# A four-layer conditioned residual stack: shifts 2 and 9 as small fp32 tiles, tiles of one width together, full copies ahead of high halves

## The chip, the cores and the metric

One NeuronCore of a Trainium2 chip runs the whole program. The metric is device time in microseconds, as the median of several runs; lower is better. The engines are named as in the profile: PE is TensorE (matmuls), PEld its weight loads, ACT is ScalarE, DVE VectorE, POOL GpSimd, SP SyncE, which issues the DMAs.

## What is computed

The input x is 128 samples of 128 channels by 2048 time steps, in fp32. Four layers follow one another, each added to its own input:

```
x = x + mix(x, cond; L0)     # agg_w[b] @ x + agg_b[b],  agg_w[b] = sum_k att[b,k] * weight[k],
                             # att = softmax(two gelu layers and a linear one on cond)
x = x + conv(x, cond; L1)    # grouped 1-d convolution, 4 groups of 32 channels, 9 taps, pad 4,
                             # plus c_weight @ cond and a bias
x = x + mix(x, cond; L2)
x = x + conv(x, cond; L3)
```

The residual is folded into the weights (an identity is added to each mixing matrix and to the centre tap).

## The kernel before

**Layout.** Layers 0 and 1 work on y1, the output of the first mix, and so on: y1 (after layer 0), y2 (after layer 1), y3 (after layer 2), o (after layer 3). For the convolutions time is split into 4 phases (t = 4m + p), so that a tile is 128 channels by 4 phases by 512 columns, with a halo column at either side. A convolution's output has the partitions (phase, channel of the group), 4 x 32, and one PSUM bank for each of the 4 channel groups. With 9 taps and 4 phases there are 12 shifts s = 0 to 11; shift s feeds output phase p where 0 <= s - p < 9. So shifts 3 to 8 feed all four phases, shifts 2 and 9 three, 1 and 10 two, 0 and 11 one.

**Two kinds of matmul in a convolution.** `dense` (L347 to L363) handles the shifts in `DENSE`, 2 to 9: value and weight are each split in a high and a low part of the type fp32r, and three products are summed (`PASSES`: high x high, high x low, low x high). Each matmul has 32 rows (one channel group) and 128 columns (all phases), and streams 512 columns; the four channel groups lie in the four row groups of the array. That is 8 shifts x 3 passes x 4 groups = 96 matmuls. `sparse` (L332 to L345) handles the shifts in `SPARSE`: plain fp32, 32 rows by 64 columns (two phases), from the unsplit copies `y1_full` and `y3_full`, in two lots: shifts 1 and 10, then shifts 0 and 11 (of whose 64 columns half meet zero weights). Each lot is 4 groups x 2 units = 8 matmuls, which use the whole array, and each fp32 matmul stands in the trace as two instructions. Below, a "pass" is one of these two over all tiles of a lot, so a lot has two passes.

**A step.** Samples are pipelined three deep. `steps`, a hardware loop (`Fori`, i = 3 to 125) and `last_steps` run `step(i)`. On PE it has this order, which nothing but the code's order sets: `first_mix(i)` (fp32, 128x128, 4 matmuls = 8 instructions, L314) into banks 0 to 3; layer 3's convolution of sample i-2, sparse lots first, then dense, into banks 4 to 7; `second_mix(i-1)` (48 fp32r matmuls of 32x128, L329) into banks 0 to 3; layer 1's convolution of sample i, dense first, then the sparse lots, into banks 4 to 7.

**The other engines in a step.** ACT reads banks: `high(1, i-1)` writes the four high parts of y2 (L477), then, for each of four banks of the first mix, a full copy (L476) and a high part (L477) of y1, then `o_ph` (L514, four banks of layer 3), then a full copy and a high part of y3 for each of four banks. DVE subtracts: the low parts of y2 straight from the banks (`low_from_bank`, L609), those of y1 and y3 from the full copies (`low`, L615), and builds the next mixing matrices between (`matrix`, L573 and L578, twice in a step; `halves`, L585 and L587). SP regroups o by 16 DMAs in a step, loads `m_parts`, x, and stores. POOL copies biases and puts o in order of time.

**Semaphores.** `high_set[l]`, `low_set[l]`: counts of high and low parts written of layer l. `mm[l]`: banks finished. Bank 4+t is free for layer 3's convolution when `low_set[1]` has counted t+1 low parts of y2, since DVE reads the bank last (`free3`, L369). A bank of the first mix may be overwritten by the second when `high_set[0]` has counted it, a bank of the second mix by the next first mix when `high_set[2]` has.

At the program's end `last_regroup` (L415) moves the last o by 16 fp32 matmuls of 32x32 tiles, and at its start `keep_busy` (L256) issues filler matmuls.

Of the kernel before, what the change touches and what calls it, by code (L numbers as in the profile page):

```python
# [5 lines left out]
def build_cond_resid(nc, x, small, mix_w, mix_b, conv_w, consts, scratch, out):  # L6
# [7 lines left out]
    PH = 4  # L14
    G = 4
# [8 lines left out]
    DENSE = range(2, SHIFTS - 2)  # L24
    SPARSE = (((1, 0, 2), (10, 2, 2)),
              ((0, 0, 2), (11, 2, 2)))
# [5 lines left out]
    with ctx:  # L32
# [12 lines left out]
        y3_full = sb("y3_full", [128, PH, HALO])  # L45
        o_ph = sb("o_ph", [128, G, N])
# [87 lines left out]
        full_first = sem("full_first")  # L134
# [117 lines left out]
        def _(pe):  # L252
# [26 lines left out]
            keep_busy(3)  # L279
# [12 lines left out]
            def side_bias():  # L292

                pe.wait_ge(ctx_in, 16)
                pe.wait_ge(full_first, 2)
# [7 lines left out]
            def first_mix(i, inner):  # L303
# [7 lines left out]
                for q in range(G):  # L311
                    if inner or i >= 2:
                        pe.wait_ge(high_set[2], nth(i - 2, q))
                    nc.tensor.matmul(ps[:, q, :], m_sum[0][:], x_t[:, q, :], start=True, stop=True).then_inc(mm[0], 1)  # L314

            def second_mix(i, inner):

                pe.wait_ge(m_in, 16 * G * i)
                for g in range(G):
                    pe.wait_ge(low_set[1], nth(i - 1, g))  # L320
                    for n, (m, a) in enumerate(PASSES):
                        first, final = g == 0 and n == 0, g == G - 1 and n == len(PASSES) - 1
                        for p in range(PH):
                            rows = slice(CG * p, CG * (p + 1))
                            if first and has(i, inner, 0):
                                pe.wait_ge(high_set[0], nth(i, p))
                            elif first:
                                pe.wait_ge(high_set[2], nth(i - 2, p))
# [37 lines left out]
            def step(i, inner):  # L366
                now, last, before = has(i, inner, 0), has(i, inner, 1), has(i, inner, 2)

                def free3(t):  # L369
                    if last:  # L370
# [4 lines left out]
                def free1(t):  # L375
                    if before:
                        pe.wait_ge(phases_set, nth(i - 2, t))
                    elif last:
# [19 lines left out]
                if now:  # L398
# [5 lines left out]
                    if not inner and i == 0:  # L404
                        side_bias()
                        pe.wait_ge(full_first, G)
# [18 lines left out]
        def _(act):  # L425
# [43 lines left out]
            def high(layer, j, k, src, dst, full=None):  # L469
# [4 lines left out]
                column = bias[layer][:, k % WIDTH[layer]:k % WIDTH[layer] + 1]  # L474
                if full is not None:
                    nc.scalar.activation(full, src, ACT.Identity, bias=column)  # L476
                nc.scalar.activation(dst, src, ACT.Identity, bias=column).then_inc(high_set[layer], 1)  # L477

            def full_of_first():

                for q in range(G):
                    act.wait_ge(low_set[0], q + 1)
                    nc.scalar.activation(segment(y1_full, q), by_phase(q), ACT.Identity, bias=bias[0][:, 0:1]).then_inc(full_first, 1)

            def step(i, inner):
                now, last, before = has(i, inner, 0), has(i, inner, 1), has(i, inner, 2)
                if last:
                    if inner or i > 1:
                        act.wait_ge(mm[2], 4 * (i - 1))
                    for g in range(G):  # L490
                        high(1, i - 1, g, ps[:, 4 + g, :], y2[:, HIGH, g, :])
                if not inner and i == 0:
                    for q in range(G):
                        high(0, i, q, by_phase(q), segment(y1[:, HIGH], q))
# [301 lines left out]
```

## Time and profile before

| what | value |
|---|---|
| median of 3 runs | 2832.29 us (2830.95 to 2833.19) |
| the profiled execution, time | 2832.44 us |
| the same, span in the trace | 2830.7 us |
| PE busy | 2809.9 us (99%) |
| DVE / ACT / POOL busy | 1961.1 / 1833.8 / 865.7 us |
| dense matmuls (L361) | 24576, 1504.8 us busy |
| sparse matmuls (L343) | 8192 instructions, 509.0 us busy |
| first mix (L314), second mix (L329) | 473.6 us, 384.1 us |
| HBM traffic | 126 GB/s over the span |

Busy shares are averages over the span. "Idle before" is the time an engine stood still ahead of a group, with what ended that. In the timeline, several instructions of one form are merged in one line with their count; its length runs to a modelled end of the last matmul, which laps over the next line's start, so stages are best measured from start to start.

### The profile page before, as it was taken

What the parts mean: (1) busy time and instruction counts of PE and PEld (TensorE: products, weight loads), DVE (VectorE), ACT (ScalarE), POOL (GpSimd) and SP (SyncE); (2) the same over time, 40 slices, a digit from 0 to 9 for tenths busy, and PEclk for the clock granted to TensorE, in tenths of its full rate; (3) what the DMA queues carried; (4) which work ended last, traced back from release to release, by engine and by line L of the source; (5) the groups of instructions that cost most, each with busy time, mean ns of one, the idle gap of its engine ahead of it and who ended that gap; (6) DMA issues with size and microseconds to landing.
All of it is one profiled execution on the core that took longest, in us unless ns stands there. A gap on an engine that the chain in (4) does not pass through costs nothing.

```text
span 2830.7 us, 101562 instructions
## 1 busy us (share of the span) xinstructions
PE 2809.9 (99%) x40052; PEld 1951.1 (69%) x40052; DVE 1961.1 (69%) x2327; ACT 1833.8 (65%) x3101; POOL 865.7 (31%) x1039
## 2 busy tenths in 40 slices
PE   9999999999999999999999999999999999999998
PEld 6667766776677667766776677667766776677665
DVE  6677667766776677667766776677667766776674
ACT  5666666666666666666666666666666666666664
POOL 1233223322332233223322332233223322322332
PEclk9999999999999999999999999999999999999999
DMA  4555555555555555555555555555555555555554
GB/s 138 172 181 179 170 169 181 179 170 169 183 176 170 169 182 177 170 169 182 177 170 170 181 177 170 170 181 178 170 171 180 178 170 171 179 178 170 171 180 139
DMA packets 228036, 489.68 MB, mean 173 GB/s; under 512 B 47016, under 2 KB 129072, under 8 KB 195376
## 3 DMA queue, kind: packets, MB, share of 16 engines
q1 hardware_dynamic: 228016, 489.39, 54.6%
q8 instruction: 15, 0.25, 0.0%
q14 instruction: 5, 0.04, 0.0%
HBM read 205.04 MB, written 150.99 MB: 126 GB/s over the span
## 4 chain that ended last, share of the span: by engine, by line
PE 99%; ACT 1%; DVE 0%; issue 0%; DVEq 0%; ACTq 0%
PE ps L361 52%; PE ps L343 17%; PE ps L314 16%; PE ps L329 13%; ACT y L477 0%; ACT y_full L476 0%; PE ps L256 0%; PE ps L261 0%; PE ps L298 0%; DVE x_t L653 0%; PE ps L415 0%; DVE y L609 0%; ACT L438 0%; DVE conv_parts L548 0%; ACT o_ph L514 0%
## 5 line engine op out<-in xcount | busy, mean ns | idle before, releaser
L361 PE MATMUL ps<-y,conv_parts 32*128 32x512 f32 x24576 | 1504.8, 392 | 1.3 <-DVE y L609 1.0
L361 PEld LDWEIGHTS ps<-y,conv_parts 32*128 32x128 f32 x24576 | 1301.0, 183 | 235.5 <-issue 105.7
L477 ACT ACTIVATE y<-ps,bias 128x512 fp32r<-128x512 f32 x1536 | 1051.4, 712 | 368.8 <-PE ps L343 355.5
L615 DVE TENSOR_TENSOR y<-y_full,y 128x512 fp32r<-128x512 f32 x1020 | 797.5, 810 | 432.4 <-ACT y L477 432.3
L685 POOL COPY bias<-bias_table 128x4 f32 (+3 forms) x512 | 199.6, 404 | 1945.3 <-DMA o_ch<-o_ph 1324.5
L476 ACT ACTIVATE y_full<-ps,bias 128x512 f32<-128x512 f32 x1020 | 733.7, 719 | 26.7 <-PE ps L329 25.0
L691 POOL COPY o_t<-o_ch 128x512 f32<-128x512 f32 x508 | 691.4, 1483 | 10.1 <-DMA o_ch<-o_ph 10.1
L514 ACT ACTIVATE o_ph<-ps,bias 128x512 f32<-128x512 f32 x510 | 309.3, 689 | 581.5 <-PE ps L361 581.5
L609 DVE SCALAR_TENSOR_TENSOR y<-ps,bias,y 128x512 fp32r<-128x512 f32 x516 | 351.8, 744 | 373.8 <-ACT y L477 373.7
L343 PE MATMUL ps<-y_full,conv_raw 32*64 32x512 f32 x8192 | 509.0, 601 | 6.6 <-ACT y L477 4.9
L314 PE MATMUL ps<-x_t,m_sum 128*128 128x512 f32 x1024 | 473.6, 605 | 0.6 <-ACT bias_table L467 0.6
L573 DVE TENSOR_TENSOR prod<-mix_sb,att_table 128x1152 f32<-128x1152 f32 x254 | 416.6, 1640 | 0.0
L329 PE MATMUL ps<-y,m_parts 32*128 32x512 f32 x6144 | 384.1, 392 | 2.3 <-ACT y L477 2.3
L314 PEld LDWEIGHTS ps<-x_t,m_sum 128*128 128x128 f32 x1024 | 184.0, 189 | 287.5 <-issue 287.5
L578 DVE TENSOR_REDUCE m_sum<-prod 128x128 f32<-128x1152 f32 x256 | 346.4, 1353 | 20.2
L343 PEld LDWEIGHTS ps<-y_full,conv_raw 32*64 32x64 f32 x8192 | 151.9, 130 | 279.3 <-issue 179.1
L329 PEld LDWEIGHTS ps<-y,m_parts 32*128 32x128 f32 x6144 | 300.5, 184 | 62.9 <-ACT y L477 2.9
L587 DVE TENSOR_TENSOR m_own<-m_sum,m_own 128x128 fp32r<-128x128 f32 x128 | 37.4, 292 | 4.4
L585 DVE CAST m_own<-m_sum 128x128 fp32r<-128x128 f32 x128 | 29.1, 227 | 15.8
L648 DVE TENSOR_SCALAR o_ph<-ps,bias 128x512 f32<-128x512 f32 x2 | 1.4, 746 | 8.9 <-PE ps L361 8.9
L256 PE MATMUL ps<-y 128*128 128x512 f32 x12 | 5.6, 596 | 1.5 <-DVE y L590 1.5
L457 ACT ACTIVATE bias_table<-ps,room 128x128 f32<-128x128 f32 x8 | 2.3, 491 | 6.2 <-PE ps L298 6.2
(53 smaller groups left out, 59.0 us busy)
## 6 DMA issues: line engine op xcount, KB each, us to landing
x_t<-x SPq DMA_DIRECT2D x128, 1024.0 KB, 5.0
o_ch<-o_ph SPq DMA_DIRECT2D x2032, 64.0 KB, 2.0
out<-o_t SPq DMA_DIRECT2D x127, 1024.0 KB, 3.9
m_parts<-mixed SPq DMA_DIRECT2D x512, 128.0 KB, 2.6
mixed<-m_own SPq DMA_DIRECT2D x128, 128.0 KB, 1.8
conv_raw<-conv_w SPq DMA_DIRECT2D x2, 768.0 KB, 10.3
mix_sb<-mix_w SPq DMA_DIRECT2D x2, 576.0 KB, 8.0
out<-x_t SPq DMA_DIRECT2D x4, 256.0 KB, 2.2
```

Source lines behind the costliest of these rows:

```text
L314: nc.tensor.matmul(ps[:, q, :], m_sum[0][:], x_t[:, q, :], start=True, stop=True).then_inc(mm[0], 1)
L329: ins = nc.tensor.matmul(ps[:, p, :], m_parts[rows, g, m, :], y2[rows, a, g, :], start=first, stop=final)
L343: ins = nc.tensor.matmul(ps[CG * p:CG * (p + width), 4 + t, :], conv_raw[layer][rows, 128 * s + CG * p:128 * s + CG * (p + width)], src[ro ...
L361: ins = nc.tensor.matmul(ps[:, 4 + t, :], conv_parts[layer][rows, w, s - DENSE[0], :], src[rows, a, p_in, q:q + N], start=first, stop=final)
L476: nc.scalar.activation(full, src, ACT.Identity, bias=column)
L477: nc.scalar.activation(dst, src, ACT.Identity, bias=column).then_inc(high_set[layer], 1)
L514: nc.scalar.activation(o_ph[:, g, :], ps[:, 4 + g, :], ACT.Identity, bias=bias[3][:, g:g + 1]).then_inc(phases_set, 1)
L573: nc.vector.tensor_tensor(prod[layer][:], mix_sb[layer][:], att.broadcast_to([128, C, K + 1]), ALU.mult).then_inc(scaled[layer], 1)
L578: nc.vector.tensor_reduce(m_sum[layer][:], prod[layer][:], AX_X, ALU.add).then_inc(summed[layer], 1)
L609: nc.vector.scalar_tensor_tensor(out=dst, in0=src, scalar=bias[layer][:, k % WIDTH[layer]:k % WIDTH[layer] + 1], in1=high.bitcast(fp32), o ...
L615: nc.vector.tensor_tensor(dst, full, high.bitcast(fp32), ALU.subtract).then_inc(low_set[layer], 1)
L691: nc.gpsimd.tensor_copy(ov[:, p, :], o_ch[:, p, :]).then_inc(in_time_set, 1)
```

## The change

Five things are done.

1. `DENSE` shrinks to shifts 3 to 8: 6 x 3 x 4 = 72 matmuls of 32x128. `conv_parts` shrinks with it.
2. `sparse` gets three lots: two `WIDE` ones of 32x64 tiles (shifts 1 and 10; shifts 2 and 9, two phases of each) and one `NARROW` one of sixteen 32x32 tiles (shift 0 for phase 0, shift 9 for phase 1, shift 2 for phase 2, shift 11 for phase 3, for each of four groups). Where the sparse part begins the convolution (layer 3), the wide lots come first, else (layer 1) the narrow one.
3. The fourth bank of layer 1 (t = 3, bank 7) is read once: ACT writes a full copy `y2_full`, the high part is made from that copy in SBUF, and DVE makes the low part from both. `free3` and `free1` wait for that bank on the full copy.
4. For y1 and y3, ACT writes all four full copies first and then the four high parts, from the full copies. What waited for the bank's release on `high_set[0]` and `high_set[2]` waits on `full_set`.
5. `keep_busy(3)` at the start becomes `keep_busy(5)`.

```diff
-    DENSE = range(2, SHIFTS - 2)
-    SPARSE = (((1, 0, 2), (10, 2, 2)),
-              ((0, 0, 2), (11, 2, 2)))
+    DENSE = range(PH - 1, SHIFTS - PH + 1)
+    WIDE = (((1, 0, 2), (10, 2, 2)), ((2, 0, 2), (9, 2, 2)))
+    NARROW = (((0, 0, 1), (9, 1, 1), (2, 2, 1), (11, 3, 1)),)
...
-            keep_busy(3)
+            keep_busy(5)
...
-                        pe.wait_ge(high_set[2], nth(i - 2, q))
+                        pe.wait_ge(full_set[2], nth(i - 2, q))
...
-                for r, units in enumerate(SPARSE):
+                lots = WIDE + NARROW if begins else NARROW + WIDE
+                for r, units in enumerate(lots):
...
-                            final = r == len(SPARSE) - 1 and not begins
+                            final = r == len(lots) - 1 and not begins
...
                 def free3(t):
-                    if last:
+                    if last and t == G - 1:
+                        pe.wait_ge(full_set[1], i)
+                    elif last:
                         pe.wait_ge(low_set[1], nth(i - 1, t))
...
-                    pe.wait_ge(high_set[2], 4 * (i - 1))
+                    pe.wait_ge(full_set[2], 4 * (i - 1))
                     sparse(3, y3_full, True, free3)
...
-            def high(layer, j, k, src, dst, full=None):
+            def from_bank(layer, j, k, src, dst, done):
...
-                column = bias[layer][:, k % WIDTH[layer]:k % WIDTH[layer] + 1]
-                if full is not None:
-                    nc.scalar.activation(full, src, ACT.Identity, bias=column)
-                nc.scalar.activation(dst, src, ACT.Identity, bias=column).then_inc(high_set[layer], 1)
+                nc.scalar.activation(dst, src, ACT.Identity,
+                                     bias=bias[layer][:, k % WIDTH[layer]:k % WIDTH[layer] + 1]).then_inc(done[layer], 1)
+
+            def high_of_full(layer, count, full, dst):
+
+                act.wait_ge(full_set[layer], count)
+                nc.scalar.copy(dst, full).then_inc(high_set[layer], 1)
...
-                    for g in range(G):
-                        high(1, i - 1, g, ps[:, 4 + g, :], y2[:, HIGH, g, :])
+                    for g in range(G - 1):
+                        from_bank(1, i - 1, g, ps[:, 4 + g, :], y2[:, HIGH, g, :], high_set)
+                    from_bank(1, i - 1, G - 1, ps[:, 3 + G, :], y2_full[:], full_set)
+                    high_of_full(1, i, y2_full[:], y2[:, HIGH, G - 1, :])
...
-                        high(2, i - 1, p, ps[:, p, :], y3[:, HIGH, p, 1:N + 1], y3_full[:, p, 1:N + 1])
+                        from_bank(2, i - 1, p, ps[:, p, :], y3_full[:, p, 1:N + 1], full_set)
+                    for p in range(PH):
+                        high_of_full(2, nth(i - 1, p), y3_full[:, p, 1:N + 1], y3[:, HIGH, p, 1:N + 1])
```

On PE, layer 3's convolution in the loop's body, before (L343 is `sparse`, L361 `dense`; `REGISTER_ALU` works out a count to wait for; the count of an entry is in kernel matmuls, so 16 fp32 ones are 32 instructions of the trace):

```order
L343 MATMUL ps<-y_full,conv_raw 64x512 [waits low_set1]
L343 MATMUL ps<-y_full,conv_raw 64x512
L371 REGISTER_ALU
L343 MATMUL ps<-y_full,conv_raw 64x512 [waits low_set1]
L343 MATMUL ps<-y_full,conv_raw 64x512 x9
L361 MATMUL ps<-y,conv_parts 128x512 [waits low_set2]
L361 MATMUL ps<-y,conv_parts 128x512 x95
```

The same place now (L345 is `sparse`, L363 `dense`):

```order
L345 MATMUL ps<-y_full,conv_raw 64x512 [waits low_set1]
L345 MATMUL ps<-y_full,conv_raw 64x512
L345 MATMUL ps<-y_full,conv_raw 64x512 [waits full_set1]
L345 MATMUL ps<-y_full,conv_raw 64x512 x9
L345 MATMUL ps<-y_full,conv_raw 32x512 x16
L363 MATMUL ps<-y,conv_parts 128x512 [waits low_set2]
L363 MATMUL ps<-y,conv_parts 128x512 x71
```

Sixteen 32-column matmuls stand between the wide ones and the dense ones, of which there are 24 fewer; the fourth bank's wait names the full copy.

On ACT, the y1 part of the loop's body, before (L476 writes the full copy, L477 the high part, both from PSUM):

```order
L476 ACTIVATE y_full<-ps,bias 128x4x128 [waits bias_set0]
L477 ACTIVATE y<-ps,bias 128x4x128
L471 REGISTER_ALU
L476 ACTIVATE y_full<-ps,bias 128x4x128 [waits mm0]
L477 ACTIVATE y<-ps,bias 128x4x128
L471 REGISTER_ALU
L476 ACTIVATE y_full<-ps,bias 128x4x128 [waits mm0]
L477 ACTIVATE y<-ps,bias 128x4x128
```

And now (L480 reads a bank, L486 copies from SBUF), with the end of the y2 part ahead of it:

```order
L486 CAST y<-y_full 128x512 [waits full_set1]
L513 REGISTER_ALU
L477 ISA [waits mm1]
L479 REGISTER_ALU [waits mm0]
L480 ACTIVATE y_full<-ps,bias 128x4x128 [waits bias_set0]
L477 REGISTER_ALU
L480 ACTIVATE y_full<-ps,bias 128x4x128 [waits mm0]
L477 REGISTER_ALU
L480 ACTIVATE y_full<-ps,bias 128x4x128 [waits mm0]
L477 REGISTER_ALU
L480 ACTIVATE y_full<-ps,bias 128x4x128 [waits mm0]
L486 CAST y<-y_full 128x4x128 [waits full_set0] x4
```

The four bank reads stand together, the four high parts behind them, and the fourth bank of layer 1 has one bank read and one copy.

## Rows read from the trace of the kernel before

**Rows 1.** The page, parts 1 and 4: busy time by engine, and the last chain.
```profile
PE 2809.9 (99%) x40052; PEld 1951.1 (69%) x40052; DVE 1961.1 (69%) x2327; ACT 1833.8 (65%) x3101; POOL 865.7 (31%) x1039
...
PE 99%; ACT 1%; DVE 0%; issue 0%; DVEq 0%; ACTq 0%
```

**Rows 2.** Windows by stage: length, busy PE PEld DVE ACT POOL, PEclk, DMA, GB/s.
```profile
1401.28:1404.91 3.63, 3.63 (x16) 1.44 (x8) 2.80 (x5) 3.52 (x7) 0.47 (x2) 1.00 0.54 136
1404.91:1406.82 1.91, 1.91 (x34) 0.59 (x33) 1.83 (x1) 1.91 (x5) 1.91 (x2) 1.00 1.05 217
1406.82:1412.52 5.70, 5.70 (x107) 4.81 (x102) 5.66 (x6) 1.62 (x3) 4.22 (x5) 1.00 0.67 277
1412.52:1415.32 2.80, 2.80 (x52) 2.33 (x47) 2.22 (x4) 2.40 (x4) 0.00 (x0) 1.00 0.44 164
1415.32:1421.14 5.82, 5.82 (x100) 5.39 (x94) 2.78 (x4) 4.77 (x9) 0.19 (x1) 1.00 0.43 113
...
1401.28:1423.04 21.76, 21.76 (x320) 15.14 (x312) 15.28 (x18) 14.22 (x24) 6.79 (x8) 1.00 0.57 175
```

**Rows 3.** Timeline: start, us, engine, line, operation, tiles, count, idle before.
```profile
1404.91 0.23 PEld L343 LDWEIGHTS ps<-y_full,conv_raw 32*64 32x64 f32 x16 [0.76 <-DVE y L609]
...
1406.82 5.44 PEld L361 LDWEIGHTS ps<-y,conv_parts 32*128 32x128 f32 x96 [0.81 <-issue]
...
1421.14 0.23 PEld L343 LDWEIGHTS ps<-y_full,conv_raw 32*64 32x64 f32 x16 [0.35 <-issue]
```

**Rows 4.** Windows, L343 on PE alone: length, busy (matmuls begun), clock, DMA, GB/s.
```profile
1404.90:1405.00 0.10, 0.09 (x8) 1.00 0.74 236
...
1404.90:1405.50 0.60, 0.58 (x16) 1.00 0.82 242
...
1404.90:1405.95 1.05, 1.03 (x24) 1.00 0.86 244
```

**Rows 5.** Windows, L415 on PE alone (32x32 tiles, the program's end).
```profile
2823.70:2824.15 0.45, 0.44 (x16) 1.00 0.77 309
...
2823.70:2824.25 0.55, 0.54 (x28) 1.00 0.93 372
```

**Rows 6.** Timeline, the same regroup and the copy that waits for it.
```profile
2823.71 1.15 PE L415 MATMUL ps<-o_ph,consts_sb 32*32 32x512 f32 x32 [1.67 <-DVE o_ph L648]
2825.43 2.03 ACT L521 COPY x_t<-ps 64x512 f32<-64x512 f32 x4 [2.08 <-PE ps L415]
```

**Rows 7.** Timeline of the same step: ScalarE, VectorE, and SyncE's last load.
```profile
1401.39 2.42 ACT L477 ACTIVATE y<-ps,bias 128x512 fp32r<-128x512 f32 x4 [2.89 <-PE ps L343]
...
1402.11 2.73 DVE L609 SCALAR_TENSOR_TENSOR y<-ps,bias,y 128x512 fp32r<-128x512 f32 x4 [2.89 <-ACT y L477]
1402.92 1.80 SPq L203 DMA_DIRECT2D m_parts<-mixed  x4
...
1408.13 3.46 DVE L615 TENSOR_TENSOR y<-y_full,y 128x512 fp32r<-128x512 f32 x4
...
1412.92 2.43 ACT L514 ACTIVATE o_ph<-ps,bias 128x512 f32<-128x512 f32 x4 [4.48 <-PE ps L361]
...
1420.29 0.69 DVE L615 TENSOR_TENSOR y<-y_full,y 128x512 fp32r<-128x512 f32 x1 [0.46 <-ACT y L477]
```

**Rows 8.** Timeline, second mix of sample 0: its first four matmuls wait one by one.
```profile
36.63 0.46 PE L329 MATMUL ps<-y,m_parts 32*128 32x512 f32 x1 [0.39 <-ACT y L477]
...
40.01 4.30 PE L329 MATMUL ps<-y,m_parts 32*128 32x512 f32 x44 [0.66 <-ACT y L477]
```

**Rows 9.** Last convolution's wait (timeline), and its clock (windows).
```profile
2812.67 3.59 PE L343 MATMUL ps<-y_full,conv_raw 32*64 32x512 f32 x32 [4.86 <-ACT y L477]
...
2812.60:2816.00 3.40, 3.33 (x32) 0.88 (x32) 0.69 (x1) 0.01 (x1) 0.00 (x0) 0.50 0.41 101
```

**Rows 10.** Timeline of the start, PE: the place of the two added filler matmuls.
```profile
7.68 0.94 PE L256 MATMUL ps<-y 128*128 128x512 f32 x3
9.61 0.72 PE L282 MATMUL ps<-att_sb,consts_sb 128*128 128x8 f32 x4 [0.99 <-DVE att_sb L600]
```

More of the change, by code:

```diff
@@ L45, in build_cond_resid @@
         y3_full = sb("y3_full", [128, PH, HALO])
+        y2_full = sb("y2_full", [128, N])
         o_ph = sb("o_ph", [128, G, N])
@@ L132, in build_cond_resid @@
         mm = [sem(f"mm{l}") for l in range(NL)]
-        full_first = sem("full_first")
+        full_set = [sem(f"full_set{l}") for l in range(3)]
         high_set = [sem(f"high_set{l}") for l in range(3)]
@@ L294, in side_bias @@
                 pe.wait_ge(ctx_in, 16)
-                pe.wait_ge(full_first, 2)
+                pe.wait_ge(full_set[0], 2)
                 for l in range(2):
@@ L377, in free1 @@
                         pe.wait_ge(phases_set, nth(i - 2, t))
+                    elif last and t == G - 1:
+                        pe.wait_ge(full_set[1], i)
                     elif last:
@@ L482, in full_of_first @@
                     act.wait_ge(low_set[0], q + 1)
-                    nc.scalar.activation(segment(y1_full, q), by_phase(q), ACT.Identity, bias=bias[0][:, 0:1]).then_inc(full_first, 1)
+                    nc.scalar.activation(segment(y1_full, q), by_phase(q), ACT.Identity, bias=bias[0][:, 0:1]).then_inc(full_set[0], 1)
             def step(i, inner):
@@ L489, in step @@
                         act.wait_ge(mm[2], 4 * (i - 1))
-                    for g in range(G):
-                        high(1, i - 1, g, ps[:, 4 + g, :], y2[:, HIGH, g, :])
+                    for g in range(G - 1):
+                        from_bank(1, i - 1, g, ps[:, 4 + g, :], y2[:, HIGH, g, :], high_set)
+                    from_bank(1, i - 1, G - 1, ps[:, 3 + G, :], y2_full[:], full_set)
+                    high_of_full(1, i, y2_full[:], y2[:, HIGH, G - 1, :])
                 if not inner and i == 0:
                     for q in range(G):
-                        high(0, i, q, by_phase(q), segment(y1[:, HIGH], q))
+                        from_bank(0, i, q, by_phase(q), segment(y1[:, HIGH], q), high_set)
                         if q == 1:
@@ L503, in step @@
                     for q in range(G):
-                        high(0, i, q, by_phase(q), segment(y1[:, HIGH], q), segment(y1_full, q))
+                        from_bank(0, i, q, by_phase(q), segment(y1_full, q), full_set)
+                    for q in range(G):
+                        high_of_full(0, nth(i, q), segment(y1_full, q), segment(y1[:, HIGH], q))
                 if before:
@@ L619, in step @@
                 if last:
-                    for g in range(G):
+                    for g in range(G - 1):
                         low_from_bank(1, i - 1, g, y2[:, LOW, g, :], ps[:, 4 + g, :], y2[:, HIGH, g, :])
+                    low(1, i - 1, G - 1, y2[:, LOW, G - 1, :], y2_full[:], y2[:, HIGH, G - 1, :])
                 if not inner and i == 0:
@@ L698, in step @@
                 if now and (inner or i + 1 < B):
-                    if not inner and i == 0:
-                        pool.wait_ge(full_first, G)
-                    pool.wait_ge(high_set[0], 4 * (i + 1))
+                    pool.wait_ge(full_set[0], 4 * (i + 1))
                     set_bias(0, i + 1)
```

8 lines of the change are left out of this document (4 added, 4 removed).

## The prediction, made before the changed kernel ran

> **What bounds the kernel now.** I read the page first. PE is busy 99% of the span and the chain that ended last is 99% PE, while DVE and ACT stand at 69% and 65% [rows 1]. So time is PE's instruction stream, as long as nobody keeps it waiting. Next, one step in the middle of the loop, cut into windows at the starts of PE's stages [rows 2]: first mix 3.63 us, layer 3's sparse part 1.91, its dense part 5.70, second mix 2.80, layer 1's dense part 5.82, and what is left of 21.76, 1.90, is layer 1's sparse part. PE's busy time equals the length of each window: there is no gap to win in a step, only work to shorten. The clock was granted at 1.00 in all of them. The program makes 128 such steps' worth of work, 256 convolutions.
>
> **The price of a wave of dense work.** Dense matmuls go in waves of four, one for each row group. Two stages of this form follow each other without a change of tile shape, 24 waves and 12 waves in 5.70 + 2.80 us: 0.236 us a wave [rows 2]. The bounds are the second mix alone, 2.80/12 = 0.233, and layer 1's dense part, 5.82/24 = 0.243. The change takes out two of eight shifts, 6 waves: 6 x 0.236 = 1.42 us off each convolution (1.40 to 1.46).
>
> **The price of a pass of fp32 work.** The first mix has 8 passes on one tile in 3.63 us, the sparse part 4 passes on eight tiles in 1.91 us: (3.63 - 1.91)/4 = 0.43 us a pass, and 0.19 us are left over in both [rows 2]. The counts agree: 8 matmuls begun by 0.10 us, 16 by 0.60, 24 by 1.05 [rows 4]. I read the 0.19 as the cost of a change of shape: weight loads, which elsewhere run ahead, stand still 0.76, 0.81 and 0.35 us where the shape changes [rows 3]. The last of these is a change of columns alone (32x128 to 32x64), the nearest to the new change from 64 to 32 columns.
>
> **The narrow lot, which no row shows in its place.** It has two passes on sixteen tiles, and makes one more change of shape. The nearest rows are the regroup at the program's end, sixteen fp32 matmuls in the same 32x32 tiles: its first 16 instructions were begun by 0.45 us and 12 more by 0.55 [rows 5]. So sixteen tiles do run beside each other, and the second pass begins at the pace of wider tiles, 0.1 us spent on starting sixteen instead of 0.05 on eight. I take 2 x 0.43 + 0.19 + 0.03 = 1.08 us. The lower bound is the passes alone, 0.86, if going from 64 to 32 columns costs nothing. The upper bound comes from the same regroup: the copy that waits for it began at 2825.43, 0.57 us after the modelled end 2823.71 + 1.15 [rows 6]; if all of that were slow streaming, a lot would be 1.65. I stay at 1.08, since the starts of rows 5 are measured and that end is modelled.
>
> On this the Trainium skill has a rule that speaks against the change: "TensorEngine Tiling (Array Packing)", Key Properties, says that changing the tiling mode drains the engine. The trace agrees for the changes that it has (the 0.19 us above). By that rule the lot costs 1.08; were a change of columns not such a change, 0.86.
>
> **The convolutions.** 1.42 - 1.08 = 0.34 us less for each, 256 x 0.34 = 87 us. The second wide lot replaces the old second lot one for one: same tiles, same 8 matmuls, no cost. By stages a step should be 3.63, 2.99, 4.28, 2.80, 4.40 and 2.98: 21.08 us.
>
> **The reordered copies, and whether the cover holds.** They move no PE work, so in the loop I cost them at nothing, and ask only who would be late. I count from the first mix's start at 1401.28. Before, DVE's last low part of y2 ended at 3.56 and layer 3's sparse part began at 3.63 [rows 2, 7]: that was tight, but on time. Now the fourth bank is free when ACT has read it, at 2.53, and the low part made from the copy is needed only by the second mix. ACT has one instruction more in a step, a copy of some 0.57 us (the pace of four of L477: 2.42 us with the last one's own length in it). It pushes y1's eight operations, and with them the low parts of y1, from 10.3 to about 10.9 [rows 7]; layer 1's dense part, which needs them, now begins at 13.70 instead of 14.04. Margin 2.8 us. Behind the new self-wait of ACT (the copy waits for the full copy) stand only these same operations. `o_ph`: ACT was idle 4.48 us before it and takes 2.43 us, against 2.80 of second mix until its banks are wanted [rows 2, 7]; idle shrinks to about 3.6, the rest is as before. y3: all four banks are free after four operations instead of eight, the last low part (20.98 - 1.28 = 19.7 before) is wanted at 21.08 + 6.62. SP's queue: its last loads, `m_parts`, were issued by 1404.72, 7.8 us ahead of the second mix; they hang on `o_ph`, whose place moves by 0.34 while the step shrinks by 0.68, so 7.1 us stay. POOL's biases wait for the full instead of the high copy, which is earlier. The least margin is thus 2.8 us.
>
> **The two ends.** In the second mix of sample 0 the four first matmuls wait for ACT one by one, 3.38 us from the first to the fourth, two ACT operations between neighbours [rows 8]; now one: 1.7 us less. The last sample's layer 3 waited 4.86 us for eight ACT operations at some 0.57 us each [rows 9]; four now: 2.3 us less. The clock stood at 0.50, the lower of its two levels, in the 3.40 us after this idle time; should the shorter idle time keep it up, another 1.7 us. The two fillers added at the start cost some 0.31 us each (three took 0.94) and fall into PE's 0.99 us of idle time behind them [rows 10]: nothing. I take 5 us for the ends (4 to 8).
>
> **Sum.** The profiled execution took 2832.44 us with a span of 2830.7, and lies on the median, 2832.29; I use that. 2832.3 - 87 - 5 = 2740 us. Its own range, with 0.233 to 0.243 a wave, 1.00 to 1.15 a narrow lot, and the ends: 2718 to 2765.
>
> **Rivals.**
> - *The change of columns costs nothing.* The lot is 0.86: 256 x 0.22 = 56 us less, 2684 us. For it: the rows are the same 32 in both lots, and no row shows this change. Against: rows 3 show a standstill where columns alone change.
> - *Cover lost.* ACT's longer y2 part and the grouped high parts make y1's low parts, or the second mix's data, late in each step. It decides only beyond 2.8 us; if 0.2 to 0.6 us were left over in each of 128 steps, the time would be 2766 to 2817 us. Against: every margin above. For: ACT and DVE slow each other in places (the four of L615 took 3.46 us where single ones take 0.69 [rows 7]).
> - *Sixteen tiles stream slower than eight*: slower than before. Sixteen moving streams instead of eight must be read for each pass. From a lot of 1.08 + 92/256 = 1.44 us on, the gain is gone; at the bound of 1.65 the time is 2740 + 256 x 0.57 = 2886 us. For it: rows 6. Against: a tile's second instruction began 0.45 us after its first in rows 5, which a slow first pass would not allow, and each of the sixteen matmuls of the regroup signals a semaphore, which those of the narrow lot don't.
> - *PE's issue sets the pace.* All stages show 58 to 60 ns for an instruction: 5.70/96, 2.80/48, 1.91/32. If this were issue, 32 narrow instructions would take 1.92 us plus 0.19 for the change of shape: 2740 + 256 x 1.03 = 3004 us. Against: 12 matmuls of the regroup were begun within 0.10 us [rows 5], 8 of the sparse part too [rows 4].
> - *No net effect*: a lot of about 1.42 us.
>
> Two statements of "TensorE: Matmul & The Clock Gate" bear on these. Its section Back-to-back issue gap gives about 62 ns for each matmul when PE's hardware decode is off; by this rule 32 instructions are an estimated 1.98 us, and the time is near the 3004 of the fourth rival; rows 5 speak against it. Its section on the per-tile semaphore tail would give an estimated 0.52 us for 16 tiles with 16 increments, close to the 0.57 of rows 6, which takes away the third rival's only evidence.
>
> **Chances.** Forecast 0.70; no cost of the columns' change 0.10; cover lost 0.08; no net effect 0.02; slower streams 0.08; issue pace 0.02. A measurement of this kernel tells 0.2% (5.7 us) from no change. Faster: 0.70 + 0.10 + 0.08 = 0.88; same 0.02; slower 0.10. The range takes in the forecast's own, the rival at 2684, and the nearer half of the lost cover: 2680 to 2785, in all some 0.84.
>
> **What would show it.** In the changed kernel's windows: dense parts of 4.28 and 4.40 us; sparse parts of 2.99 and 2.98, with a standstill of weight loads ahead of the narrow lot, and 16 narrow matmuls begun within about 0.1 us; a step of 21.08. A narrow lot over 1.44 us, or PE idle ahead of a stage in the loop (layer 1's dense part first), would prove the forecast wrong; a narrow lot of 0.86 would make it too high. At the end, PE's wait before the last convolution should fall from 4.86 to about 2.5 us.

## The result, and the profile after

| | before | changed |
|---|---|---|
| median | 2832.74 us (2830.95 to 2833.61, 4 runs) | 2753.03 us (2751.88 to 2753.49, 4 runs) |
| span of the profiled execution | 2830.7 us | 2750.1 us |

The ratio of the changed kernel's time to that before is 0.9713 (95% interval 0.97 to 0.9725): 79.7 us less. The forecast was 2740 us, with 2718 to 2765 as its own range.

The page of the changed kernel, parts 1 and 4, against [rows 1]:

```profile
PE 2731.4 (99%) x42102; PEld 1708.3 (62%) x42102; DVE 1954.8 (71%) x2327; ACT 1852.1 (67%) x3229; POOL 978.5 (36%) x1039
...
PE 98%; DVE 1%; SPq 0%; ACT 0%; issue 0%; DMA 0%; DVEq 0%
```

PE is still what the time consists of. The windows by stage, against [rows 2] (length, then busy time of PE, PEld, DVE, ACT, POOL, granted clock, DMA share, GB/s; the stages are first mix, layer 3 sparse, layer 3 dense, second mix, layer 1 dense, layer 1 sparse, and the whole step):

```profile
1402.12:1405.75 3.63, 3.63 (x13) 1.44 (x9) 2.55 (x4) 3.56 (x7) 0.27 (x1) 1.00 0.47 122
1405.75:1408.78 3.03, 3.03 (x67) 0.88 (x66) 2.90 (x4) 3.03 (x7) 3.03 (x3) 1.00 0.75 209
1408.78:1413.03 4.25, 4.25 (x77) 3.62 (x76) 4.25 (x5) 0.87 (x2) 4.18 (x5) 1.00 0.46 193
1413.03:1415.83 2.80, 2.80 (x52) 2.33 (x47) 2.64 (x3) 2.39 (x4) 0.00 (x0) 1.00 0.93 377
1415.83:1420.27 4.44, 4.44 (x76) 4.00 (x69) 1.66 (x5) 4.27 (x9) 0.26 (x1) 1.00 0.42 104
1420.27:1423.30 3.03, 3.03 (x65) 0.99 (x64) 1.22 (x3) 0.24 (x1) 0.00 (x0) 1.00 0.48 130
1402.12:1423.30 21.18, 21.18 (x332) 13.25 (x328) 15.22 (x18) 14.37 (x25) 7.74 (x8) 1.00 0.56 180
```

A step takes 21.18 us instead of 21.76. The forecast had 3.63, 2.99, 4.28, 2.80, 4.40 and 2.98, in all 21.08. Over 116 steps of the trace (first mix to first mix, 109.66 to 2567.39 us) the mean is 21.19 us; before it was 21.76 over 112 (117.45 to 2554.56 us). 128 steps give 73 us; the rest, some 6 to 7 us, lies at the two ends.

The timeline's weight loads, against [rows 3] (start, length, engine, line, operation, tiles, count, idle before):

```profile
1407.65 0.29 PEld L345 LDWEIGHTS ps<-y_full,conv_raw 32*32 32x32 f32 x32 [0.81 <-issue]
1408.77 3.99 PEld L363 LDWEIGHTS ps<-y,conv_parts 32*128 32x128 f32 x72 [0.84 <-issue]
...
1420.27 0.23 PEld L345 LDWEIGHTS ps<-y_full,conv_raw 32*32 32x32 f32 x32 [0.35 <-issue]
1421.34 0.29 PEld L345 LDWEIGHTS ps<-y_full,conv_raw 32*64 32x64 f32 x16 [0.84 <-issue]
```

Weight loads stand still 0.81 and 0.84 us around the narrow lot: a change of columns from 64 to 32, or back, is a change of shape like the others. The lot takes 1.12 us from one start to the next in layer 3 (1.07 in layer 1, where the wide lots behind it take the rest).

At the program's end, against [rows 9], in the timeline and in a window:

```profile
2728.61 2.42 ACT L480 ACTIVATE y_full<-ps,bias 128x512 f32<-128x512 f32 x4 [0.43 <-issue]
...
2731.09 3.10 PE L345 MATMUL ps<-y_full,conv_raw 32*64 32x512 f32 x64 [2.55 <-ACT y_full L480]
...
2731.00:2735.00 4.00, 3.91 (x80) 1.67 (x84) 2.50 (x4) 2.10 (x5) 0.00 (x0) 1.00 0.42 103
```

PE waits 2.55 us before the last convolution instead of 4.86, and the clock stays at the upper of its levels behind it, where it had been at 0.50.

The second mix of sample 0 as it is now, against [rows 8], and then the last stores, before (at 2826.15) and now (at 2743.45):

```profile
33.73 4.72 PE L330 MATMUL ps<-y,m_parts 32*128 32x512 f32 x48 [0.16 <-DVE y L630]
...
35.38 2.64 PEld L330 LDWEIGHTS ps<-y,m_parts 32*128 32x128 f32 x45 [0.40 <-ACT y_full L480]
...
2826.15 2.16 SPq L243 DMA_DIRECT2D out<-x_t  x4
...
2743.45 3.83 SPq L244 DMA_DIRECT2D out<-x_t  x4
```

The weights of that mix's fourth matmul are loaded 1.7 us behind the start of the first; before, the fourth began 3.38 us behind it. This is the 1.7 us less of the forecast. But the program's last stretch got longer: from the start of the last regroup on PE (2823.71 before, 2740.56 now) to the end of the span it is 7.0 us before and 9.5 now, and the row of the last four stores on SyncE's queue is 3.83 us long instead of 2.16. The same stretch is 7.0 us in the run with the tiles alone below and 7.8 in the one with the copies alone; why it is longer was not tested. The forecast had no term for it; it takes some 2.5 us off what the ends gain.

### The profile page after: what moved, and what is told of

It is laid out like the page before. It is cut to its first block, busy times and chain, and to the rows that moved or that the text cites. A ratio compares the mean times of both kernels' runs of the same rounds, so it can differ in the third digit from the quotient of the medians.

```text
span 2750.1 us, 105789 instructions
## 1 busy us (share of the span) xinstructions
PE 2731.4 (99%) x42102; PEld 1708.3 (62%) x42102; DVE 1954.8 (71%) x2327; ACT 1852.1 (67%) x3229; POOL 978.5 (36%) x1039
## 4 chain that ended last, share of the span: by engine, by line
PE 98%; DVE 1%; SPq 0%; ACT 0%; issue 0%; DMA 0%; DVEq 0%
PE ps L363 40%; PE ps L345 28%; PE ps L315 17%; PE ps L330 13%; SPq L211 0%; PE ps L257 0%; ACT y L480 0%; DVE y L630 0%; DVE y L624 0%; DMA o_ch<-o_ph 0%; PE ps L299 0%; PE ps L262 0%; DVE x_t L669 0%; PE ps L421 0%; ACT y L486 0%
## 5 line engine op out<-in xcount | busy, mean ns | idle before, releaser
L630 DVE TENSOR_TENSOR y<-y_full,y 128x512 fp32r<-128x512 f32 x1148 | 950.0, 881 | 402.6 <-ACT y L486 402.6
L363 PE MATMUL ps<-y,conv_parts 32*128 32x512 f32 x18432 | 1143.0, 392 | 1.3 <-ACT att_table L455 0.5
L363 PEld LDWEIGHTS ps<-y,conv_parts 32*128 32x128 f32 x18432 | 973.4, 183 | 204.0 <-issue 107.2
L345 PE MATMUL ps<-y_full,conv_raw 32*32 32x512 f32 (+1 forms) x16384 | 794.5, 599 | 4.2 <-ACT y_full L480 2.5
L707 POOL COPY o_t<-o_ch 128x512 f32<-128x512 f32 x508 | 753.1, 1609 | 10.6 <-DMA o_ch<-o_ph 10.6
L480 ACT ACTIVATE y_full<-ps,bias 128x512 f32<-128x512 f32 x1148 | 706.8, 689 | 23.2 <-PE ps L330 21.5
L486 ACT CAST y<-y_full 128x512 fp32r<-128x512 f32 x1148 | 640.4, 639 | 4.1
L345 PEld LDWEIGHTS ps<-y_full,conv_raw 32*32 32x32 f32 (+1 forms) x16384 | 238.8, 116 | 472.8 <-issue 375.5
L624 DVE SCALAR_TENSOR_TENSOR y<-ps,bias,y 128x512 fp32r<-128x512 f32 x388 | 267.6, 744 | 332.4 <-ACT y L480 332.3
L480 ACT ACTIVATE y<-ps,bias 128x512 fp32r<-128x512 f32 x388 | 238.7, 685 | 362.7 <-PE ps L345 349.4
L588 DVE TENSOR_TENSOR prod<-mix_sb,att_table 128x1152 f32<-128x1152 f32 x254 | 342.8, 1349 | 0.0
L602 DVE TENSOR_TENSOR m_own<-m_sum,m_own 128x128 fp32r<-128x128 f32 x128 | 37.4, 292 | 4.4
```

Of the source, the lines that this page charges most:

```text
L345: ins = nc.tensor.matmul(ps[CG * p:CG * (p + width), 4 + t, :], conv_raw[layer][rows, 128 * s + CG * p:128 * s + CG * (p + width)], src[ro ...
L363: ins = nc.tensor.matmul(ps[:, 4 + t, :], conv_parts[layer][rows, w, s - DENSE[0], :], src[rows, a, p_in, q:q + N], start=first, stop=final)
L480: nc.scalar.activation(dst, src, ACT.Identity, bias=bias[layer][:, k % WIDTH[layer]:k % WIDTH[layer] + 1]).then_inc(done[layer], 1)
L486: nc.scalar.copy(dst, full).then_inc(high_set[layer], 1)
L588: nc.vector.tensor_tensor(prod[layer][:], mix_sb[layer][:], att.broadcast_to([128, C, K + 1]), ALU.mult).then_inc(scaled[layer], 1)
L624: nc.vector.scalar_tensor_tensor(out=dst, in0=src, scalar=bias[layer][:, k % WIDTH[layer]:k % WIDTH[layer] + 1], in1=high.bitcast(fp32), o ...
```

## The experiments

### The tiles without the copies, and the copies without the tiles

The first is the kernel before with this edit alone:

```diff
-    DENSE = range(2, SHIFTS - 2)
-    SPARSE = (((1, 0, 2), (10, 2, 2)),
-              ((0, 0, 2), (11, 2, 2)))
+    DENSE = range(PH - 1, SHIFTS - PH + 1)
+    WIDE = (((1, 0, 2), (10, 2, 2)), ((2, 0, 2), (9, 2, 2)))
+    NARROW = (((0, 0, 1), (9, 1, 1), (2, 2, 1), (11, 3, 1)),)
...
-                for r, units in enumerate(SPARSE):
+                lots = WIDE + NARROW if begins else NARROW + WIDE
+                for r, units in enumerate(lots):
```

> The kernel before with the new tiles only: dense shifts 3 to 8, two wide lots and a narrow one; copies, their order, their semaphores and the fillers as before. Theory (the copies act at the program's two ends only): the same step of 21.18 us, and some 4 to 5 us more at the ends: 2757 to 2758 us. Rival (the fourth bank, which became free only 0.07 us before it was wanted, now makes PE wait in each step, or the banks of the mixes do): a step of 21.3 or more, 2770 us or more.

Measured: 2761.12 us (2760.19 to 2762.84), ratio 0.9732 (0.9716 to 0.9749) against its own runs of the kernel before. Its timeline, PE at layer 1's dense part of two neighbouring steps and at the end, and two windows:

```profile
1400.65 4.51 PE L362 MATMUL ps<-y,conv_parts 32*128 32x512 f32 x72
...
1421.85 2.52 PE L362 MATMUL ps<-y,conv_parts 32*128 32x512 f32 x39
...
2740.54 4.89 PE L344 MATMUL ps<-y_full,conv_raw 32*64 32x512 f32 x64 [4.87 <-ACT y L478]
...
40.00:44.00 4.00, 4.00 (x44) 3.12 (x40) 3.90 (x6) 0.00 (x0) 0.00 (x0) 0.50 0.01 6
2741.00:2745.00 4.00, 4.00 (x64) 0.88 (x48) 0.22 (x1) 0.00 (x0) 0.00 (x0) 0.56 0.40 98
```

The step is 21.20 us here (21.19 as a mean over 115), as in the changed kernel: the tiles alone give the whole gain of the loop, and the bank that came free just in time didn't become a wait. The ends cost 8 us more by the two medians and by the two spans (2758.4 and 2750.1 us), but only 5 by the two ratios, against 4 to 5 expected: the runs of the kernel before stood 5 us higher beside this run (2838.03 us) than beside the changed kernel's. The old wait of 4.87 us is back, 2.3 us more than 2.55, and so is the lower clock, near 40 us and behind that wait. So the copies, with the two fillers that this run also lacks, are worth 5 to 8 us in a program with the new tiles; 2.3 us are that wait, 1.7 the mix of sample 0, and part of the rest is the clock.

The second is the changed kernel with `DENSE`, the two lots of `SPARSE` and `keep_busy(3)` of before.

> The changed kernel with the old tiles (dense shifts 2 to 9, two wide lots) and three fillers: only the copies and their order are new. Theory: a step of 21.76 us as before, 4 us off at the ends: about 2828 to 2829 us. Rival (part of the 80 us comes from the copies): 2820 us or less. Other rival (the extra copy makes someone late): over 2833 us.

Measured: 2830.35 us (2829.53 to 2833.05), ratio 0.9979 (0.9969 to 0.9989). The runs of the kernel before that it is compared with spread from 2831.36 to 2840.78 us, so the size is less sure than the interval says; the two spans are 2828.3 and 2830.7 us. Its step, from layer 3's sparse part on:

```profile
1402.73 1.97 PE L344 MATMUL ps<-y_full,conv_raw 32*64 32x512 f32 x32
1404.64 5.86 PE L362 MATMUL ps<-y,conv_parts 32*128 32x512 f32 x96
1410.33 2.98 PE L330 MATMUL ps<-y,m_parts 32*128 32x512 f32 x48
1413.14 5.90 PE L362 MATMUL ps<-y,conv_parts 32*128 32x512 f32 x96
1418.97 1.97 PE L344 MATMUL ps<-y_full,conv_raw 32*64 32x512 f32 x32
```

From start to start, the four stages that can be read here are those of [rows 2] within 0.01 us, and the mean step is 21.77 us (112 steps, first mix to first mix, 114.48 to 2553.09 us). The copies do nothing in the loop, a few microseconds at the ends.

### One change of shape more

```diff
-                lots = WIDE + NARROW if begins else NARROW + WIDE
+                lots = WIDE[:1] + NARROW + WIDE[1:]
```

> The changed kernel with the narrow lot put between the two wide ones in both convolutions: same tiles and passes, one change of shape more in each convolution. Theory: 0.20 to 0.26 us more for each of 256 convolutions, 51 to 67 us: 2804 to 2820 us. Rival (the excess belongs to the narrow tiles): no change, 2753 us.

Measured: 2803.98 us (2 runs, 2803.8 and 2804.17), 51 us more than the changed kernel, 0.20 for each convolution. The weight loads of layer 3's sparse part, and of the dense part behind it:

```profile
1409.47 0.23 PEld L345 LDWEIGHTS ps<-y_full,conv_raw 32*64 32x64 f32 x16 [0.76 <-DVE y L624]
1410.52 0.29 PEld L345 LDWEIGHTS ps<-y_full,conv_raw 32*32 32x32 f32 x32 [0.81 <-issue]
1411.65 0.23 PEld L345 LDWEIGHTS ps<-y_full,conv_raw 32*64 32x64 f32 x16 [0.84 <-issue]
1412.69 3.99 PEld L363 LDWEIGHTS ps<-y,conv_parts 32*128 32x128 f32 x72 [0.81 <-issue]
```

Each lot now stands alone between two changes of shape: the wide ones take 1.05 and 1.04 us (two passes, 0.86, and 0.19), the narrow one 1.13. So of the narrow lot's price 0.19 is the change, and only 0.08 belongs to its sixteen tiles, where I had 0.03.

### No change of shape inside the sparse part

If a change costs 0.19 us, a sparse part all in 32x32 tiles should be cheaper with the same six passes:

```diff
-    WIDE = (((1, 0, 2), (10, 2, 2)), ((2, 0, 2), (9, 2, 2)))
-    NARROW = (((0, 0, 1), (9, 1, 1), (2, 2, 1), (11, 3, 1)),)
+    WIDE = ()
+    NARROW = (((0, 0, 1), (1, 1, 1), (2, 2, 1), (9, 3, 1)),
+              ((1, 0, 1), (2, 1, 1), (9, 2, 1), (10, 3, 1)),
+              ((2, 0, 1), (9, 1, 1), (10, 2, 1), (11, 3, 1)))
```

(The waits for the banks stand ahead of the 32x32 matmuls as instructions of their own, and `mm[1]` counts 16 for a sample.)

> The changed kernel, but all of the sparse part in 32x32 tiles: three lots of sixteen, each with one shift for each of the four output phases, no 64-column tiles, so the change of shape inside the sparse part is gone. Six passes as before. Theory (a change of shape costs about 0.2 us wherever it stands, sixteen tiles stream at 0.43 us a pass): a sparse part of 6 x 0.43 + 0.19 + 0.05 = 2.82 us instead of 3.03, a step of 20.76 instead of 21.18, 54 us less: about 2699 us. Rival (the narrow lot's 1.12 us is the slower streaming of sixteen tiles): 3 x 1.12 = 3.36 us, a step of about 21.8, about 2838 us.

Measured: 2852.86 us (2852.62 to 2853.02), 100 us more than the changed kernel. My theory of the price was wrong for lots that follow each other. The windows on L348, PE alone, from the start of layer 1's sparse part (in brackets the matmuls begun), and the weight loads of the same stretch:

```profile
1405.60:1405.80 0.20, 0.17 (x16) 1.00 0.88 312
1405.60:1406.20 0.60, 0.57 (x32) 1.00 0.62 215
...
1405.60:1407.00 1.40, 1.38 (x49) 1.00 0.46 141
...
1405.62 0.23 PEld L348 LDWEIGHTS ps<-y_full,conv_raw 32*32 32x32 f32 x32 [0.35 <-issue]
1406.08 0.10 PEld L348 LDWEIGHTS ps<-y_full,conv_raw 32*32 32x32 f32 x1 [0.22 <-issue]
1406.51 0.55 PEld L348 LDWEIGHTS ps<-y_full,conv_raw 32*32 32x32 f32 x32 [0.33 <-issue]
1407.37 0.75 PEld L348 LDWEIGHTS ps<-y_full,conv_raw 32*32 32x32 f32 x31 [0.31 <-issue]
```

The first lot runs as forecast: 32 loads in 0.23 us, sixteen matmuls begun at once, sixteen more 0.45 us later. The second lot's loads come 0.89 us after the first's, not one pass ahead, and take 0.55 us, and its sixteen matmuls are spread over 0.4 us. The whole part is 3.34 us: 1.1 us for every lot behind the first. The rival's number (2838) was nearer, but its reason is wrong: the streams themselves are not slow, since the second pass of the first lot still begins some 0.45 us behind the first.

### The narrow lot twice

```diff
-                lots = WIDE + NARROW if begins else NARROW + WIDE
+                lots = WIDE + NARROW * 2 if begins else NARROW * 2 + WIDE
```

> The changed kernel with the narrow lot issued twice in a row in each convolution; the second adds shifts 0, 9, 2 and 11 a second time, so the output is not the reference's. Theory (only the first narrow lot behind a change of shape finds its weights loaded; the second runs at the slower pace seen in the kernel of three narrow lots, 1.1 us): 256 x 1.1 = 282 us more, about 3035 us. Rival (two passes at 0.43): 220 us more, about 2973 us.

Measured: 3049.14 us (one run), 296 us more, 1.16 for each added lot, though it brings no change of shape. The loads of layer 1's two narrow lots and of the wide one behind them:

```profile
1407.14 0.23 PEld L345 LDWEIGHTS ps<-y_full,conv_raw 32*32 32x32 f32 x32 [0.35 <-issue]
1407.60 0.10 PEld L345 LDWEIGHTS ps<-y_full,conv_raw 32*32 32x32 f32 x1 [0.22 <-issue]
1408.03 0.55 PEld L345 LDWEIGHTS ps<-y_full,conv_raw 32*32 32x32 f32 x31 [0.32 <-issue]
1409.42 0.23 PEld L345 LDWEIGHTS ps<-y_full,conv_raw 32*64 32x64 f32 x16 [0.84 <-issue]
```

The same late and slow loading. A second narrow lot costs 1.16 us and a first one, with its change of shape, 1.12.

### Four wide lots

The changed kernel with no 32x32 tile; shifts 0, 11, 2 and 9 are padded to two phases by zero weights.

```diff
-    WIDE = (((1, 0, 2), (10, 2, 2)), ((2, 0, 2), (9, 2, 2)))
-    NARROW = (((0, 0, 1), (9, 1, 1), (2, 2, 1), (11, 3, 1)),)
+    WIDE = (((1, 0, 2), (10, 2, 2)), ((2, 0, 2), (9, 2, 2)),
+            ((0, 0, 2), (11, 2, 2)), ((9, 0, 2), (2, 2, 2)))
+    NARROW = ()
```

> The changed kernel without 32x32 tiles: shifts 0, 1, 2, 9, 10 and 11 in four wide lots of eight 32x64 tiles, units of one phase padded to two by zero weights. One change of shape less, two passes more. Theory (a pass of eight tiles is 0.43 us, however many lots follow each other): a sparse part of 8 x 0.43 + 0.19 = 3.63 us instead of 3.03, a step of 22.38: about 2907 us. Rival (later wide lots slow down as later narrow ones do): 2940 us or more.

Measured: 2905.78 us (one run). Its layer 1 sparse part is followed by the first mix:

```profile
1409.08 3.69 PE L346 MATMUL ps<-y_full,conv_raw 32*64 32x512 f32 x64
1412.70 3.70 PE L316 MATMUL ps<-x_t,m_sum 128*128 128x512 f32 x8
```

3.62 us for eight passes: lots of eight tiles keep 0.43 us a pass however many follow each other. Without the packing of four odd units into one lot of sixteen tiles the kernel would be slower than before.

### Why later narrow lots are slow: order or number

Two explanations were at hand: loads of neighbouring tiles in one row group of the array wait for each other, or a lot of sixteen tiles is so many instructions that the next lot's loads can't be brought forward. The first was tried by exchanging the inner loops, so that neighbours lie in different row groups, in the kernel of three narrow lots and in the changed kernel:

```diff
-                    for t in range(G):
-                        rows = slice(CG * t, CG * (t + 1))
-                        if r == 0 and begins:
-                            wait_bank(t)
-                        for s, p, width in units:
+                    for s, p, width in units:
+                        for t in range(G):
+                            rows = slice(CG * t, CG * (t + 1))
+                            if r == 0 and begins and p == 0:
+                                wait_bank(t)
```

> The kernel with three narrow lots (2853 us, a sparse part of 3.34 and 3.48 us), with the same exchange of the two inner loops. Theory A (loads in one row group wait for each other): passes go back to 0.43 us, a sparse part of 2.82 us, about 2700 us. Rival B (a lot of sixteen tiles is too many instructions to load weights ahead of the pass that uses them, whatever their order): 2840 to 2860 us.

Measured: 2835.41 us (2833.74 to 2836.73). Layer 1's sparse part stays where it was, and its loads too:

```profile
1418.21 3.40 PE L348 MATMUL ps<-y_full,conv_raw 32*32 32x512 f32 x96
1421.54 2.84 PE L317 MATMUL ps<-x_t,m_sum 128*128 128x512 f32 x6
```

3.33 us. The 17 us go with layer 3, whose part fell from 3.48 to 3.34 us. In the old order each group's wait for its bank stood ahead of its four matmuls; now all four stand at the lot's start. That this is the reason was not tested apart. The order of the tiles doesn't cure the loads.

> The changed kernel, with the two inner loops of the sparse part exchanged: within a lot the four channel groups (row groups of the array) come innermost, so neighbouring matmuls and weight loads lie in different row groups. Theory A (weight loads of neighbouring small tiles in one row group wait for each other, which makes the narrow lot 0.09 us dearer than a wide one with its own change of shape, and slows later narrow lots): up to 0.09 us less for each convolution, 2730 to 2750 us. Rival B (the order within a lot does not matter, since each pass has 0.43 us for its starts): 2753 us, within 3.

Measured: 2755.07 us (2754.65 to 2755.38), ratio 0.972 (0.9705 to 0.9735): no difference that can be told from the changed kernel's.

The number was tried by cutting lots of sixteen in lots of eight. The first try didn't separate the two:

```diff
-    NARROW = (((0, 0, 1), (9, 1, 1), (2, 2, 1), (11, 3, 1)),)
+    NARROW = (((0, 0, 1), (9, 1, 1)), ((2, 2, 1), (11, 3, 1)))
```

> The changed kernel with the narrow lot cut in two lots of eight 32x32 tiles (shifts 0 and 9, then 2 and 11), one after the other. Theory (a lot slows down behind another when it has sixteen tiles, 64 instructions with their weight loads; with eight it doesn't): four passes at 0.43 and one change of shape, 1.91 us instead of 1.12, 202 us more: about 2955 us. Rival (32x32 tiles are slow behind each other whatever their number): the second lot takes 1.15 us, the pair 2.27, 294 us more: about 3047 us.

Measured: 2751.86 us (one run), as fast as the changed kernel. Both my numbers were wrong for the same reason: the two halves use different column groups of the array, so they are the same sixteen tiles, begun in another order, and run beside each other. So lots count as behind each other only where they use the same tiles, however the code writes them.

The second try puts lots of eight on the same tiles behind each other: the kernel of three narrow lots with phases 0 and 1 first (three lots), then phases 2 and 3.

```diff
+    NARROW = (((0, 0, 1), (1, 1, 1)), ((1, 0, 1), (2, 1, 1)), ((2, 0, 1), (9, 1, 1)),
+              ((2, 2, 1), (9, 3, 1)), ((9, 2, 1), (10, 3, 1)), ((10, 2, 1), (11, 3, 1)))
```

(`start` and `stop` are set for each half of three lots, and the waits for the banks are instructions of their own, as above.)

> The kernel with the whole sparse part in 32x32 tiles, reordered: three lots of eight tiles follow each other on the column groups of phases 0 and 1, then three on those of phases 2 and 3. Two lots on the same tiles have 32 instructions between them instead of 64, as wide lots do. The fourth lot can run beside the third. Theory (small tiles keep 0.43 us a pass behind each other when a lot has eight of them): the starts within the first three lots lie 0.43 us apart, 10 passes or so in all, a sparse part of 4.3 to 4.5 us. Rival (32x32 tiles are slow behind each other whatever their number): starts 0.5 us apart or more from the second lot on, a sparse part of 5.2 us or more.

Measured: 3187.21 us (one run), a sparse part of 4.72 us. That lies between the two numbers. The start of it, in windows and in the loads:

```profile
1421.40:1421.80 0.40, 0.38 (x8) 1.00 0.89 312
1421.40:1422.20 0.80, 0.78 (x16) 1.00 0.53 178
1421.40:1422.60 1.20, 1.18 (x24) 1.00 0.54 163
...
1421.42 0.18 PEld L347 LDWEIGHTS ps<-y_full,conv_raw 32*32 32x32 f32 x16 [0.35 <-issue]
1421.88 0.15 PEld L347 LDWEIGHTS ps<-y_full,conv_raw 32*32 32x32 f32 x8 [0.28 <-issue]
1422.31 0.15 PEld L347 LDWEIGHTS ps<-y_full,conv_raw 32*32 32x32 f32 x8 [0.28 <-issue]
1422.61 0.97 PEld L347 LDWEIGHTS ps<-y_full,conv_raw 32*32 32x32 f32 x33 [0.15 <-issue]
```

The second lot on the same small tiles is loaded one pass ahead and begins on time: loads at 1421.88 and 1422.31, 0.43 us apart, as wide lots have them. So small tiles are not slow behind each other as such. The irregular stretch from 1422.61 on is where the fourth lot, on other tiles, comes in while the third waits; there sixteen tiles would be at work again, and the pace is lost; I read this from the order of the code, no row shows which tile a load is for. The Trainium skill ("TensorE: Matmul & The Clock Gate", The mechanism) says that PE draws weight loads ahead within a window of 64 instructions. A lot of sixteen fp32 tiles has 64, with its loads, and one of eight has 32. The rows fit this: behind lots of eight the next lot's loads come one pass ahead, behind lots of sixteen they come late. But the size of the window was not measured here, so this stays an explanation that agrees with the rows. They would also agree with a limit on how many tiles (sixteen, not eight) can be loaded ahead: in every run here the number of tiles and the number of instructions between two lots rise together, and no run separates them.

### The fillers

The changed kernel with `keep_busy(3)` again.

> The changed kernel with three fillers instead of five at the start. Theory (the two fillers keep the clock at its upper level through the start, which stood at 0.50 for 3.4 us before): a stretch at 0.50 comes back, of which up to 1.7 us are lost: 2753.5 to 2755 us. Rival (nothing on the path there): 2753 us, within 0.5.

Measured: 2754.99 us (2754.12 to 2757.87, 5 runs), ratio 0.9722 (0.9709 to 0.9736); the changed kernel's interval is 0.97 to 0.9725, so they can't be told apart. Windows at the start and near the end:

```profile
2718.00:2723.00 5.00, 5.00 (x48) 1.57 (x64) 1.82 (x3) 1.37 (x3) 1.73 (x3) 0.66 0.56 148
9.00:14.00 5.00, 4.27 (x29) 3.54 (x30) 4.39 (x8) 2.22 (x5) 0.37 (x3) 1.00 1.02 422
```

With three fillers too the clock stayed up at the start of this execution, and fell near 2719 us. My theory of the fillers is not borne out; which of the short idle times at the ends is followed by the lower clock differs between executions, and what the two fillers do stays open.

## Why the prediction was right

The time came out 13 us above the forecast, inside its range, and the mechanism was the one forecast: less PE work in every convolution, nobody late in the loop, less waiting at the ends. One thing about the range: its terms don't give its lower end. 256 x (1.46 - 1.00) = 118 us and 8 at the ends lead to 2706 us, not 2718. The upper end does come out (2764).

**The bound.** PE's stream was the bound before and after; no stage in the loop has an idle PE. Both halves of that were tested: the tiles alone give the step of 21.19 us, the copies alone leave it at 21.77.

**The wave.** Six waves were priced at 1.42 us, from 0.236 for each. Measured: 5.70 - 4.25 = 1.45 in layer 3, 5.82 - 4.44 = 1.38 in layer 1, 1.415 on average. Right.

**The pass and the change of shape.** 0.43 and 0.19 us were read off two stages. Four wide lots (8 passes, 3.62 us) and the narrow lot between the wide ones (0.20 us a convolution for one change more) confirm both numbers. The rival in which a change of columns costs nothing fell.

**The narrow lot** is the term that was mis-sized: 1.08 forecast, 3.03 - 1.91 = 1.12 measured, of which 0.07 instead of 0.03 goes to its being sixteen tiles. By stages the differences are +0.04 and +0.05 us (sparse parts), -0.03 and +0.04 (dense parts): a step is 0.10 us longer than forecast, 13 us in 128 steps, which is the distance from 2740 to 2753; the ends, 1 to 2 us better than forecast, take back little of it. The nearest row, the regroup, was the right one to go by, and its upper reading of 1.65 us (slow streams) was rightly given little weight. But what I concluded from it, that sixteen tiles stream like eight, holds only for one lot behind a change of shape. With a second narrow lot in the change, the same argument would have been wrong by 0.25 to 0.3 us a lot, as my own forecast for three narrow lots was, by 154 us.

**The cover** held, but 2.8 us was not the tightest margin. That was the one of y1's low parts against layer 1's dense part: they now end at 1412.91, and that part begins at 1415.83, 2.9 us later. The prediction's own figures have a tighter one: `o_ph` takes 2.43 of the 2.80 us until its banks are wanted, and begins some 0.4 us into them.

```profile
1408.63 4.28 DVE L630 TENSOR_TENSOR y<-y_full,y 128x512 fp32r<-128x512 f32 x4
...
1413.44 2.42 ACT L527 ACTIVATE o_ph<-ps,bias 128x512 f32<-128x512 f32 x4 [3.78 <-PE ps L363]
```

Its last copy ends at 1415.86, just when the first matmuls of layer 1's dense part begin. It was as tight before (1415.35 and 1415.32), and PE shows no idle time there in either kernel. The prediction rightly said that this place stays as it was, and then left it out when it called 2.8 us the least margin; its own 2.53 and 3.63 us for the fourth bank are closer too, 1.1 us. The evidence given for the lost cover, that ACT and DVE slow each other, was misread too: while the four L615 took 3.46 us, ACT was idle for all but the first 0.3 us [rows 7], and POOL was busy for 4.22 us of that stage [rows 2]. In the changed kernel four L630 take 4.28 us beside POOL's copies and 2.50 (at 1418.99) beside ACT's. Whether POOL is the cause was not tested.

**The ends** were put at 5 us. They are 6 to 7: the wait before the last convolution is 2.55 us (2.5 forecast), the mix of sample 0 gave its 1.7 us, and in the profiled execution no matmul runs at the lower clock any more. Against these stand the 2.5 us of the last stores, which were not foreseen. In part the sum was near by luck. The 5 us were 2.3 and 1.7 and 1 for the clock; without the stores' 2.5 the ends would have given some 9 us, so that some 5 are left for the clock and what was not taken apart. That the lower clock went with the shorter waits fits the tiles alone, where it is back, but isn't shown: with the same short waits a stretch at the lower level came back near 2719 us in the execution with three fillers, and from 37.4 to 39.1 us (granted clock 0.50) in the one with the inner loops exchanged and five fillers. How much each is worth can't be read off better than to a few microseconds.

**The rival of PE's issue** (32 instructions at 60 ns) fell: 16 narrow matmuls are begun within 0.2 us, as the first window of the kernel of three narrow lots shows.

## What to carry to other kernels

When work is moved between tile shapes, count three things apart: passes, changes of shape, and how the next lot's weights get loaded; here 0.43, 0.19 and, in lots of sixteen small tiles behind each other, 0.25 to 0.3 us more a lot. Half-used tiles are worth packing into one full lot of small ones even at the price of a change of shape, but a second such lot pays far less. Reordering copies on engines that don't bound the loop shows only where the pipeline fills and drains, and there a shorter wait may also spare the lower clock. When margins are listed to show that nobody comes late, list those that the change doesn't touch too: the tightest here was one of them.

## What the runs showed that I had not expected

- A lot of sixteen 32x32 fp32 tiles costs 1.1 to 1.16 us behind another of its kind, against 0.86 for eight 32x64 tiles of the same work. Three such lots in a row (3.34 us) are slower than two wide lots and a narrow one with their extra change of shape (3.03).
- The order in which the sixteen tiles are issued makes no difference (3.34 and 3.33 us), but with waits for banks between their groups of four the part was 0.14 us longer.
- Lots on different column groups run beside each other even where the code issues them one after the other: 2751.86 us for two half lots.
- In the tiles alone the lower clock lay in three stretches near the ends, as before; with the shorter waits and without it at any matmul the profiled execution is 8 us shorter.
- The changed kernel's last stores came 2.5 us later behind PE's last work than before, a price at the very end that the PE stages don't show.
